# Attention stage of a hybrid kernel: preparation placed between the units, scores over 32 rows in pairs of units

## The reference

```
qkv = x @ W_qkv + b_qkv
q, k, v = jnp.split(qkv, 3, axis=-1)          # 16 heads of 16 features
att = jnp.einsum('bhqd,bhkd->bhqk', q, k) / np.sqrt(HEAD_DIM)
diff = idx[:, None] - idx[None, :]
allowed = (diff >= 0) & (diff < WINDOW)       # WINDOW = 64
att = jax.nn.softmax(jnp.where(allowed[None, None], att, -jnp.inf), axis=-1)
y = jnp.einsum('bhqk,bhkd->bhqd', att, v)
return y @ W_proj + b_proj
```

## Time and profile before

| what | us |
|---|---|
| runs (three) | 2670.06, 2673.03, 2679.05 |
| median | 2673.03 |
| the profiled execution's own time | 2670.67 |
| its span, first to last instruction | 2668.9 |
| attention within it | 1982.80 to 2553.64 |

### The profile page before, as it was taken

One profiled execution on the slowest core, in us unless ns is written; L12 is line 12 of the kernel. 1 busy time (PEld: TensorE's weight loads), 2 busy tenths in 40 slices (PEclk: granted clock), 3 DMA queues, 4 the chain that ended last, 5 costly groups with the idle time before them and its releaser, 6 DMA issues. The chain is left out here.

```text
span 2668.9 us, 40685 instructions
## 1 busy us (share of the span) xinstructions
PE 2247.7 (84%) x14744; PEld 1351.1 (51%) x14744; DVE 1968.9 (74%) x2761; ACT 1856.0 (70%) x3169; POOL 1549.8 (58%) x1342
## 2 busy tenths in 40 slices
PE   0789898898998998988989989863659899988867
PEld 0345455454454554554545545532436666666644
DVE  3389889888898888898888988875635555555544
ACT  0598988888989989889899898862614433343452
POOL 1189889898898898898988988991100000000010
PEclk9899999999999999999999999985789999999989
DMA  5413404314234244042241340405020000000031
GB/s 180 103 33 87 100 26 114 85 35 112 57 71 117 66 99 99 21 119 66 55 111 41 88 99 24 116 1 180 1 102 1 17 17 17 17 17 17 17 113 63
DMA packets 125980, 180.54 MB, mean 68 GB/s; under 512 B 11218, under 2 KB 74194, under 8 KB 125396
## 3 DMA queue, kind: packets, MB, share of 16 engines
q1 hardware_dynamic: 125780, 177.94, 24.7%
HBM read 135.43 MB, written 42.47 MB: 67 GB/s over the span
## 5 line engine op out<-in xcount | busy, mean ns | idle before, releaser
L617 POOL TENSOR_TENSOR h<-h,C_rep 128x512 f32<-128x512 f32 x1024 | 1275.6, 1283 | 197.2 <-ACT h_carry L536 197.2
L423 DVE TENSOR_TENSOR_SCAN h<-decay,h_carry,psum 128x512 f32<-128x512 f32 x768 | 955.4, 1269 | 126.4 <-PE psum L745 95.4
L528 ACT ACTIVATE decay<-dt_rep,A 128x512 f32<-128x512 f32 x1024 | 729.4, 713 | 99.2 <-DVE h L423 92.2
L745 PEld LDWEIGHTS psum<-ident,u_B 128*128 128x128 f32 x4096 | 476.2, 141 | 559.2 <-DVE h L423 309.4
L745 PE MATMUL psum<-ident,u_B 128*128 128x128 f32 x4096 | 629.9, 280 | 140.1 <-DVE h L423 108.2
L548 ACT ACTIVATE u_B<-u_tok,B_tok 128x512 f32<-128x512 f32 x832 | 589.3, 710 | 63.9 <-PE psum L745 45.8
L423 DVE TENSOR_TENSOR_SCAN h<-decay,zero,psum 128x512 f32<-128x512 f32 x256 | 318.8, 1270 | 52.1 <-PE psum L745 34.7
L1412 POOL TENSOR_TENSOR a_rstd<-a_vareps,a_minushalf 128x4 f32<-128x4 f32 x9 | 9.2, 1017 | 502.9 <-DVE a_vareps L1442 502.9
L754 PE MATMUL psum<-h,state_sum 128*32 128x512 f32 x2048 | 279.7, 619 | 11.3 <-POOL h L617 10.9
L1564 ACT ACTIVATE a_probs<-a_probs 128x512 f32<-128x512 f32 x128 | 80.6, 630 | 257.6 <-DVE a_probs L1502 257.6
L606 POOL TENSOR_TENSOR u_B<-u_tok,B_tok 128x512 f32<-128x512 f32 x192 | 200.9, 1046 | 42.9 <-DVE u_tok L395 42.9
(11 more groups left out here) (201 smaller groups left out, 2826.0 us busy)
## 6 DMA issues: line engine op xcount, KB each, us to landing
dt_rep<-dt_rows SPq DMA_DIRECT2D x256, 256.0 KB, 5.5
C_rep<-C_rows SPq DMA_DIRECT2D x256, 64.0 KB, 2.0
dt_rows<-x_dt_gated SPq DMA_DIRECT2D x16, 1024.0 KB, 4.8
x_tok<-mamba_residual SPq DMA_DIRECT2D x16, 512.0 KB
residual<-mamba_residual SPq DMA_DIRECT2D x16, 512.0 KB, 3.9
mamba_residual<-residual SPq DMA_DIRECT2D x16, 512.0 KB, 2.9
a_x<-after_slots SPq DMA_DIRECT2D x9, 512.0 KB, 5.2
f_gru_weights<-in_slot_gru_dram SPq DMA_DIRECT2D x2, 2176.0 KB
```

Source lines behind the costliest of these rows:

```text
L423: dve.tensor_tensor_scan(h[:, slot(u)], dec[:, u % DEC], PS[:, u % 2], first, ALU.mult, ALU.add)\
L528: act.activation(dec[:, u % DEC], dtr[:, k % EG], ACT.Exp, scale=A[:, s // STEPS, k:k + 1]).then_inc(S["decay"], 1)
L617: pool.tensor_tensor(h[:, slot(u)], h[:, slot(u)], crep[:, k // EG], ALU.mult).then_inc(S["hc"], 1)
L745: ins = pe.transpose(PS[:, u % 2, tb * P:(tb + 1) * P], pr[:, f % 2, tb, eg], ident[:])
```

## The change

- **Scores.** q is kept once (`qF`). k is kept twice, with the even heads' features zeroed in one copy and the odd heads' in the other (`k_by_parity`), and in slots of 64 tokens (even blocks, then odd ones). A unit is now a band of 32 array rows: two neighbouring heads of the first feature tile and two of the second. One matmul meets 32 rows, 64 queries and 256 columns (two heads by 128 keys). Units are issued in pairs: two masks, then eight matmuls that alternate between the two units, so between two row bands and two PSUM banks, and between the two column halves. Four banks hold scores.
- **Preparation.** The boundary is gone. Eight steps (two blocks of transposes, two of q, two of k, two of v) follow units 7 to 14 of the chunk before, all in PSUM bank 7; each waits until the one before has been copied out. The first chunk's eight steps run before the first unit.
- **v.** It is computed once per tile; POOL makes the copy shifted by 64 tokens (`v_skewed`). The k halo is a POOL copy too. POOL also normalises x now, in place of DVE.
- **Banks.** Transposes have one bank (4), values one (5), y and the projection one (6).
- **Stores** go out per tile, 32 in all. The load of x is the first DMA.

The core of the diff (n counts units over the whole stage, u within a chunk, J tiles; in the order loop, m is the preparation step):

```diff
+    STATS, AGGR, PREP, FIN, YT, PROJ, ADD = 0, 4, 7, 7, 8, 9, 10
+    LAST = NU - HG + ADD
...
+        xnT = sb("xn_feat", [P, KT, C])
+        bk = sb("k_bias_by_parity", [P, KT, 2])
+        qF = sb("q", [P, 2, KT, C])
+        kF = sb("k_by_parity", [P, 2, KT, 2, SLOT, WIN])
...
+        V1 = sb("v_tile", [P, 2, TG, NH, HW + 1])
+        V0 = sb("v_skewed", [P, 2, TG, NH, HW + 1])
...
+                sp.dma_start(xg[:, 0], xv[0]).then_inc(ld[0], 16)
...
+                    for J in range(s * TG, (s + 1) * TG):
+                        sp.wait_ge(S["o"], J + 1)
+                        sp.dma_start(ov[J], yo[:, J % 8]).then_inc(stored[J % 8], 16)
...
+                pool.memset(V1[:, 1], 0.0).then_inc(S["init"], 1)
...
+                pool.memset(kF[:, 1], 0.0).then_inc(S["init"], 1)
...
+                    for i in range(TG):
+                        pool.tensor_scalar(xn[:, i], xg[:, k, i], mv[:, i, 0:1], rs[:, i:i + 1], ALU.subtract, ALU.mult)\
+                            .then_inc(S["xn"], 1)
...
+                    pool.tensor_copy(kF[:, s % 2, :, :, ODD], kF[:, (s - 1) % 2, :, :, ODD + TG])\
+                        .then_inc(S["kh"], 1)
...
+                    pool.tensor_copy(V0[0:WIN, k], V1[0:WIN, k]).then_inc(S["v0"], 1)
...
+                    pool.tensor_copy(V0[WIN:P, k, 1:TG], V1[WIN:P, k, 0:TG - 1]).then_inc(S["v0"], 1)
...
-                    for hh in range(FH):
-                        ins = dve.tensor_scalar(qS[:, FH + hh], PS[:, 3], W[:, A_HM + hh:A_HM + hh + 1],
-                                                bq[:, 1, hh:hh + 1], ALU.mult, ALU.add)
-                    ins.then_inc(S["q_dve"], 1)
...
+                        for e in range(2):
+                            to = kF[:, s % 2, ft, e, 0:2 * (ODD + 1)].rearrange("p (o b) w -> p o b w", o=2)[:, :, 0:TG]
+                            act.activation(to, PS[:, 7].rearrange("p (b o w) -> p o b w", o=2, w=WIN), ACT.Identity,
+                                           bias=bk[:, ft, e:e + 1], scale=W[:, A_EO + e:A_EO + e + 1]).then_inc(S["k"], 1)
...
+                def scores(n):
...
+                        pe.wait_ge(S["shift"], n - 2)
+                    m = mask[:, 0 if s % NB == 0 and j == 0 else 1]
+                    for i in range(2):
+                        pe.matmul(PS[:, (n + i) % 4].rearrange("p (h t) -> p h t", h=4), identb[:],
+                                  m.rearrange("p (o t) -> p o t", o=1).to_broadcast([P, 4, P]), start=True, stop=False)
                     for ft in range(KT):
+                        for i in range(2):
+                            rows = slice(RG * (r + i), RG * (r + i + 1))
+                                at = j * P + WIN * blk
+                                keys = kF[rows, k, ft, :, j:j + 2 * (ODD + blk)].rearrange("p e (o b) w -> p e o b w", o=2)[:, :, :, 0]
+                                ins = pe.matmul(PS[WIN * blk:WIN * (blk + 1), (n + i) % 4, ft * 2 * P:(ft + 1) * 2 * P],
+                                                qF[rows, k, ft, at:at + WIN], keys, start=False, stop=(ft == KT - 1))
+                            if ft == KT - 1:
+                                ins.then_inc(S["s_mm"], 1)
...
+                    if r == 0 and J >= 1:
+                        pe.wait_ge(S["y"], J)
...
+                for m in range(8):
+                    prepare(0, m)
+                for n in range(LAST + 1):
+                    if n < NU and n % 2 == 0:
+                        scores(n)
+                    if 2 <= n < NU + 2:
+                        transp(n - 2)
+                    if 3 <= n < NU + 3:
+                        values(n - 3)
+                    if tile_at(n, YT) is not None:
+                        y_transp(tile_at(n, YT))
+                    if tile_at(n, PROJ) is not None:
+                        project(tile_at(n, PROJ))
+                    s, m = chunk_at(n, PREP)
+                    if s and 0 <= m < 8:
+                        prepare(s, m)
```

More of the change, by code:

```diff
@@ L1311 @@
 HG = NH // 4
+RG = P // HG
 FH = P // HW
@@ L1318 @@
 A_BK = A_BQ + KT
-A_HM = A_BK + KT
-A_BV = A_HM + FH
-A_BP = A_BV + D
+A_EO = A_BK + KT
+A_BV = A_EO + 2
+A_BP = A_BV + 2 * D
 A_ALL = A_BP + D
@@ L1340, in attention @@
         identb = sb("ident_bf16", [P, P], BF16)
-        mask = sb("masks", [P, NC_, P], BF16)
+        mask = sb("masks", [P, 2, P], BF16)
         half = sb("minushalf", [P, TG])
@@ L1369, in attention, with tile_at, chunk_at @@
         ld = [signals.add(f"a_x_loaded{k}") for k in range(2)]
[L1370 to L1378, removed]
+        stored = [signals.add(f"a_stored{k}") for k in range(8)]
+        def tile_at(n, lag):
+            J, rest = divmod(n - lag, HG)
+            return J if rest == 0 and 0 <= J < NJ else None
+        def chunk_at(n, at):
+            s, u = divmod(n, U)
+            return (s + 1, u - at) if s + 1 < N and n < NU else (None, None)
         with nc.Block() as block:
@@ L1427, in _ @@
                 for ft in range(KT):
[L1428 to L1442, removed]
@@ new lines, in transp, with values @@
+                def transp(n):
+                    pe.wait_ge(S["exp"], n + 1)
+                    if n >= 1:
+                        pe.wait_ge(S["pT"], n)
+                    for i in range(4):
+                        ins = pe.transpose(PS[:, 4, i * P:(i + 1) * P], pr[:, n % 4, i], ident[:])
+                    ins.then_inc(S["p_tp"], 1)
+                def values(n):
+                    s, u = divmod(n, U)
+                    j, r = divmod(u, HG)
+                    J = s * TG + j
+                    pe.wait_ge(S["pT"], n + 1)
+                    if u == 0:
+                        pe.wait_ge(S["v0"], 3 * (s + 1))
+                    if r == 0 and J >= 1:
+                        pe.wait_ge(S["y"], J)
+                    for i in range(4):
+                        h = i // 2 * FH + 2 * r + i % 2
+                        for blk in range(2):
+                            ins = pe.matmul(PS[WIN * blk:WIN * (blk + 1), 5, h * (HW + 1):(h + 1) * (HW + 1)],
+                                            pT[:, n % 3, i, WIN * blk:WIN * (blk + 1)], (V1 if blk else V0)[:, s % 2, j, h],
+                                            start=True, stop=True)
+                    ins.then_inc(S["av"], 1)
@@ new lines, in y_transp, with project @@
+                def y_transp(J):
+                    pe.wait_ge(S["y"], J + 1)
+                    if J >= 1:
+                        pe.wait_ge(S["o"], J)
+                    for kt in range(KT):
+                        ins = pe.transpose(PS[:, 6, kt * P:(kt + 1) * P], y[:, J % 2, kt * P:(kt + 1) * P], ident[:])
+                    ins.then_inc(S["y_tp"], 1)
+                def project(J):
+                    pe.wait_ge(S["yT"], J + 1)
+                    for kt in range(KT):
+                        ins = pe.matmul(PS[:, 6, D:2 * D], yT[:, J % 2, kt], W[:, A_P + kt * D:A_P + (kt + 1) * D],
+                                        start=(kt == 0), stop=(kt == KT - 1))
+                    ins.then_inc(S["o_mm"], 1)
```

467 lines of the change are left out of this document (214 added, 253 removed).

## The result

The changed kernel takes 2595.28 us (2591.78 to 2604.57), the kernel before 2674.71 us beside it: a ratio of 0.9709, 95% interval 0.9677 to 0.9741. Faster, but by 79 us where 136 were forecast. The profiled execution took 2591.78, its span 2590.0.

The account below looks back on a forecast made before the run. TensorE was taken to bind attention by its own work. Head 40 + 8 chunks x 49.7 - 12.0 + tail 9.4 = 435.0 us instead of 570.8, so 2537 us for the kernel, range 2507 to 2596.

Parts of the forecast that it names:

- the forecast case: Whole kernel: the main mechanism holds, with POOL's and the page's prices included; 2507 to 2569 us, chance 0.75.
- What bounds the kernel: Attention before the change: TensorE binds by its own work, 2.38 us a unit without a gap.
- Preparation, scores, pair, other engines.: Per attention chunk: 46.0 us of TensorE work plus 3.7 of waits, 49.7; DVE 30 and ACT 27 us busy.
- The disputed term: Scores of a pair of units on TensorE: 1.00 us with four matmuls at a time; ends 1.00 and 3.44.
- POOL: Its work per chunk, normalising 2.4 and v copies 5.0 us, 11.4 in all, was to cost nothing.
- POOL late: Rival: POOL at twice the row's rate or more delays each chunk's first transposes; 10 us more, 2547; within the 0.75.
- Head: Attention before the first mask matmul: 40 us instead of 36.1 (36 to 46), with POOL's clearing about 9.
- The sum: Attention: 40 + 8 x 49.7 - 12.0 + 9.4 = 435.0 us instead of 570.8, 135.8 less.
- Two tiles at a time: Rival: score matmuls overlap across columns but not rows; 1.85 us a pair, 54 us more, 2591; chance 0.19.
- No overlap: Rival: every score pass runs alone; 3.44 us a pair, 156 us more, 2693; chance 0.03.
- The clock: Rival: half-filled array rows in scores count as idling and halve TensorE's clock in every chunk; about 2905 us; chance 0.02.
- list of signs: In attention's profile: pair scores 1.0 us, chunk period 49 to 50, DVE's wait largest, granted clock 0.95 or more.

Follow-up runs that it names:

- e1: Changed kernel with each score matmul reading all 128 array rows and writing 128 of its 256 columns, same passes; 2540.07 us.
- e2: Changed kernel with each score matmul reading all 128 array rows and writing all 256 columns, two tiles in flight instead of four; 2591.89 us.
- e8: Changed kernel with each unit of a pair reading its own 64 array rows instead of 32, all else the same; 2546.96 us.
- e7: Changed kernel with preparation steps after every second unit and score matmuls over all 128 rows and 128 of 256 columns; 2544.41 us.
- e3: Kernel before the change, with its score matmuls reading only array rows 0 to 63 of 128; 2761.44 us.
- e4: Changed kernel with each tile's projection, and the addition behind it, one unit later; nothing left out; 2546.23 us.
- e6: Changed kernel with preparation steps after every second unit and the projection one unit later; nothing left out; 2522.55 us.
- e5: Changed kernel with the eight preparation steps after every second unit (1, 3, ... 15) instead of units 7 to 14; 2553.73 us.
- e9: Changed kernel with two useless full-row mask matmuls added per tile, right behind its last unit's values, ahead of the wait for y; 2558.14 us.

## Why the prediction was wrong

The forecast was 2537 us, and 2595 was measured, at the very edge of the range and outside the forecast case's own (2507 to 2569). By its own steps:

- **What bounds the kernel** was right: TensorE before and after, DVE's wait for scores still the largest of the engines that compute every unit.
- **Preparation, scores, pair, other engines.** TensorE's work in an undisturbed chunk is 47.59 us (46.0 forecast), its waits 2.9 (3.7), together 50.5 (49.7). The disputed term, 1.00 us for a pair's scores, measured 1.02. Sixteen passes of 0.215 one after another, 3.44 us, thus ran 3.4 times as fast as in a row; the Trainium skill (TensorE: Matmul & The Clock Gate, Measured speedup vs the span model) gives 3.07 for four row tiles, which was the price of 8 us that the forecast left out, and rightly: here the tiles are two by two, and the trace has 1.02 us where that figure gave an estimate of 1.12.
- **POOL** was mis-sized and harmless, as argued. Normalising takes 1221 ns a tile where the rate of the earlier trace rows gave 0.6, yet TensorE's first transposes of a chunk waited for it for 0.7 us in the whole stage. The copies of v were mis-sized the other way, 2.4 us a chunk (1.08, 0.41 and 0.87) where the sum had 5.0, so that all of POOL's work is 10.6 us where 11.4 were forecast. The rival "POOL late" falls: twice the rate in normalising cost nothing.
- **Head** 35.9 us instead of 40: the clearing of 4096 columns took 3.57 us, not the 7 or so that two small memsets suggested. The 4 us too many here and some 3.5 too few at the end nearly cancel: the last chunk with the tail takes 50.65 where the sum had 49.7 - 12.0 + 9.4 = 47.1.
- **The sum** without the clock is borne out by e1, 436.2 us against 435.0, in part by errors that cancel: head and first chunk took 85.2 us there (89.7 forecast), the last chunk with the tail 50.7 (47.1).
- **Two tiles at a time** is refuted as the cause (1.02 us in the pair), though its price was good to 4 us: e2 took 2592 against 2591. Its time and the measured one agree by accident. **No overlap** is refuted by the same 1.02.
- **The clock** is the step that failed. The rival was named ("the new scores fill half of the array's rows, and if that counted as idling, all 46 us of a chunk would double") but priced only at 2905, with every chunk doubled, and at the point where no gain is left (down for 37 per cent of the time), and so given 0.02. The truth lies below both: the clock was down for 106.5 us more than in e1 (143.4 against 36.9), which cost 48.6 us of attention (484.8 against 436.2), 0.46 us for each; beside e8, whose waits are the same, it is 105.2 us and 43.9, 0.42 for each. In the profiled executions the gap is 56.9 us (2591.78 against 2534.9), and 49.9 of it lie in attention; the other 7 lie outside, where the same code ran 3.7 us longer ahead of attention and 3.4 behind it than in the kernel before. (Attention began between 1980.8 and 1991.6 us in the twelve profiles.) The forecast had the row in hand, the fall behind a half-empty stretch, and read it as something that only a boundary brings. Its list of signs did ask for it: a granted clock of 0.95 or more, and 0.85 in attention is what came.

What was the cause, then? First, array rows left empty by the scores: e1, e7, e8 fill them and the falls go or nearly; e3 empties them in another kernel and they come. Second, what stands between such scores. e4 and e6 take most or all of TensorE's waits for y away, and most falls go with the scores as they are. e5 keeps the waits and puts a step of full-row preparation behind every second unit in place of eight in a row, and e9 puts full-row work just ahead of the waits: most falls go there too. Each change by itself removes the loss or most of it (29.2 to 66.5 us at the lower clock in place of 143.4). So empty rows and short waits, in a stretch with little full-row work, together brought the falls. What stays open is how the chip weighs the three, and why the same wait is followed by a fall in one tile and not in the next.

## What to carry to other kernels

Packing small matmuls into row groups shortened them as forecast (1.02 us a pair against 1.87 in e2), but price the clock with them: count the part of the array that all matmuls in flight fill, and expect that the clock can fall where half of it is empty and TensorE also waits now and then, even for about a microsecond. Spread work that fills the rows between them (e5: 42 us). Then look for the short waits: an independent piece of TensorE work moved into one (here the projection, one unit later) paid 49 us where its wait had held 17. And where a rival is a matter of degree, price the middle, not only its two ends.

## What the runs showed of the hardware that was not expected

- Halving the rows of a matmul leaves its duration (275 ns at the upper clock, 279 before) and lowers the clock around it: 65.7 to 276.3 us at 1.2 GHz in attention, 2672 to 2761 us in all (e3).
- Two matmuls on different halves of the rows count together (e8, 38.2 us at the lower clock, against 143.4 with a quarter each).
- Idle time of 0.20 and 0.88 us in a tile, with half-empty scores, stood before 30.7 us at half speed, in which TensorE had no gap at all; added full-row work just ahead of that idle time made the kernel 37 us faster (e9).
- The four transposes in every unit did not bring the clock down: with the rows filled, chunks with eighty transposes ran at 1.00 throughout (e1).
